# A four-layer graph network on one core: row-by-row fetching by SP and ACT in the two attention sweeps as well, and PSUM operands in the spreading of logits and in two node stages

## The chip, the cores and the metric

One core of one Trainium2 chip runs the whole program in one launch. The metric is the device time of one execution in microseconds.

## What is computed

12,500 nodes with 128 features, 200,000 edges sorted by destination. Four layers, each with a LayerNorm and a ReLU ahead of it and a residual sum behind it: attention with one head (A, followed by a BatchNorm), attention with four heads and edge features (B), a layer that sums edge features and applies three dense layers (C), and a relational layer with eight weight matrices (rel). Cut to what the change touches:

```python
h = x @ W                                   # A and B: attention
e = leaky_relu(a_src[src] + a_dst[dst] (+ a_edge))
ex = exp(e - segment_max(e, dst)[dst])
out = segment_sum(ex / segment_sum(ex, dst)[dst] * h[src], dst)

agg = segment_sum(edge_attr_128, dst)       # C: its sums ride along with sweep A

h = einsum('nd,rdo->rno', x, W_rel)         # rel
out = relu(x @ W_self + b + segment_sum(h[edge_type, src], dst) / deg)
```

## The kernel before

The program is a row of stages; at the end of each, all five engines meet (`finish_stage`: a drain, one semaphore, a wait for all five): graph (indices, table A), spreading A and sweep A, nodes A (softmax ends, BatchNorm, table B), spreading B and sweep B, nodes B (with layer C and the table of rel), sweep rel, nodes rel. In each sweep every one of 200,704 (padded) edges needs the row of its source node from a table in HBM.

**Sweeps.** An edge array has 128 partitions and 1,568 columns. A sweep takes it in 98 groups of 16 columns (NG = 98, GC = 16, in two steps of 8 columns). For each column GpSimd issues one indirect DMA: 128 rows of the table, one per partition, into the tile `edge_rows` (L1077 for A and B, L2036 for rel). The tile is a ring of 5 groups in A and of 6 in B and rel. GpSimd may begin group g when the sums of group g-NS are stored and group g-NS+1 is summed. VectorE adds the groups up one after another (A and B: logits, L1213 to L1233, then the joining of steps, L1190 and L1195; in A also the edge attributes, L1165 and L1173, and the projection of the edge features, L1242 and L1252; rel: L2107 and L2121). ScalarE does the exponentials, and in A 16 scalings of a column (L1131). SP stores the sums of each group (L1111, L2052). In A it also loads, two groups ahead, the 1 MB of edge attributes (L1091) and the features (L1095). Its order in sweep A is fixed: for each g the attributes of g+2, the features of g+2 (which wait until VectorE has used those of g), the store of g (which waits until g is summed).

**Row-by-row fetching.** In sweep rel, GpSimd leaves out the last column of every second group from 7 on (`HELPED`, 45 of the 98 groups). Its 128 rows are fetched by SP and ACT, one DMA per row: `fetch_rows` loads 32 row numbers from SBUF into 32 registers (L1991) and issues 32 DMAs of one row each (L1993, L1994). SP does a quarter 4 groups ahead and one 3 groups ahead, right behind the store of the group; ACT does a quarter 2 groups ahead and one 1 group ahead. VectorE waits for the rows ahead of the group (after L2107). The row numbers stand in `helped_row`, made at the start of nodes B: a copy to float (L1874), a transpose on TensorE (L1942), a copy back to integers (L1878).

**Spreading.** Ahead of sweeps A and B the logit of a destination node, which stands at its first edge, is spread to all its edges by a scan, logit = keep * logit before + logit (L715, one per head). In B, VectorE then adds the edge terms for all heads at once (L755) and sums them along each node by four more scans (L759). All operands lie in SBUF.

**Nodes.** GpSimd gathers each node's sums in 14 chunks of 7 indirect DMAs (L1280). In nodes A and nodes B, `v_join` scales sums and own rows by the softmax factors and adds them (L1373, L1375, L1377); GpSimd may gather chunk k when chunk k-2 is joined. In nodes rel three VectorE instructions (L2154, L2156, L2158) finish a chunk. Here too all operands lie in SBUF.

## Time and profile before

| | us |
|---|---|
| three runs | 7196.33, 7212.66, 7212.68 (median 7212.66) |
| the profiled execution's own time | 7196.47 |
| its span, first to last instruction | 7194.6 |
| busy: GpSimd (POOL) | 5087.8 (71%) |
| busy: VectorE (DVE) | 3425.5 (48%) |
| busy: ScalarE (ACT) | 985.2 (14%) |
| busy: TensorE (PE) | 624.0 (9%) |
| mean granted TensorE clock | 0.54 of full speed |

Span and own time differ by 1.9 us. The busy shares are means over seven stages with different limits, so the stages have to be read apart. The DMA queues on SP and ACT are "q1" and "q10" in the profile, GpSimd's is "q0"; issuing a DMA isn't counted as busy.

### The profile page before, as it was taken

The numbers are of one execution on the slowest core, as the hardware profiler recorded it, in microseconds if no ns is written. First come the engines' busy times: TensorE is split into PE (matmuls) and PEld (weight loads), VectorE is DVE, ScalarE is ACT, GpSimd is POOL, SyncE is SP. The second block draws the span as 40 slices with busy tenths as digits, with TensorE's granted clock in tenths as the row PEclk, the third lists the DMA queues.
The fourth block names the chain that finished last, engine by engine and source line by source line (L and its number), as shares of the span: only waits on it lengthen the run. The fifth ranks groups of instructions, "written<-read, shape, count | busy, mean of one in ns | idle before, by whom it ended". The sixth has DMA issues, their size and how long they took to land. (4 is left out here: it accounts for less than half of the span.)

```text
span 7194.6 us, 39656 instructions
## 1 busy us (share of the span) xinstructions
PE 624.0 (9%) x2403; PEld 426.9 (6%) x2403; DVE 3425.5 (48%) x6202; ACT 985.2 (14%) x3082; POOL 5087.8 (71%) x5295
## 2 busy tenths in 40 slices
PE   1100000000001530000000000058411000000000
PEld 1100000000000420000000000024200000000000
DVE  8466666666666664444444444478322222222223
ACT  2122222222222120000000000056200000000000
POOL 5777777777775577777777777633477777777776
PEclk7555555555555665555555555579755555555555
DMA  5366767676765423333333333345333333333332
GB/s 182 111 213 210 224 210 225 209 226 209 225 209 180 147 98 113 115 115 115 115 115 115 115 115 115 101 160 201 139 107 108 113 108 107 110 110 107 107 112 86
DMA packets 334692, 1044.18 MB, mean 145 GB/s; under 512 B 106489, under 2 KB 128764, under 8 KB 296514
## 3 DMA queue, kind: packets, MB, share of 16 engines
q1 hardware_dynamic: 151986, 668.92, 25.9%
q0 software_dynamic: 173632, 368.42, 20.3%
q10 hardware_dynamic: 8784, 4.31, 0.2%
q14 instruction: 271, 2.22, 0.1%
q8 instruction: 19, 0.31, 0.0%
HBM read 527.27 MB, written 513.96 MB: 145 GB/s over the span
## 5 line engine op out<-in xcount | busy, mean ns | idle before, releaser
L1077 POOL DMA_INDIRECT edge_rows<-table_b,src_i x1568 | 1502.2, 958 | 477.8 <-issue 477.8
L1077 POOL DMA_INDIRECT edge_rows<-table_a,src_i x1568 | 1483.9, 946 | 477.9 <-issue 477.9
L2036 POOL DMA_INDIRECT edge_rows<-table_rel,rel_row x1523 | 1437.0, 944 | 510.3 <-issue 462.8
L2121 DVE TENSOR_TENSOR edge_rows<-edge_rows,ps 128x1024 f32<-128x1024 f32 x195 | 238.0, 1221 | 1386.9 <-DMA edge_rows<-table_rel,rel_row 1383.5
L1213 DVE TENSOR_TENSOR z<-edge_rows,dst_logit 128x16 f32<-128x16 f32 (+1 forms) x196 | 40.9, 209 | 1679.1 <-DMA edge_rows<-table_b,src_i 1026.4
L1195 DVE TENSOR_TENSOR edge_rows<-edge_rows,ps 128x1032 f32<-128x1032 f32 (+1 forms) x390 | 484.2, 1242 | 84.4 <-ACT edge_rows L1131 67.3
L1190 DVE TENSOR_TENSOR ps<-edge_rows,ps 128x1032 f32<-128x1032 f32 (+1 forms) x390 | 485.7, 1245 | 8.6 <-ACT edge_rows L1131 1.9
L1131 ACT ACTIVATE edge_rows<-edge_rows,weight_decay 128x129 f32<-128x129 f32 x1568 | 470.1, 389 | 0.0
L805 PE MATMUL ps<-ident,edge_rows 128*128 128x128 f32 x16 | 3.9, 426 | 3483.2 <-DVE edge_rows L1195 2034.1
L1134 ACT ACTIVATE ps<-weight_decay 128x128 f32<-128x128 f32 x98 | 27.5, 281 | 1893.4 <-DVE weight_decay L1233 1893.4
L2069 ACT ACTIVATE ps<-keep 128x16 f32<-128x16 f32 x98 | 19.6, 201 | 1850.7 <-DVE edge_rows L2121 1847.0
L2107 DVE TENSOR_TENSOR ps<-edge_rows,ps 128x1024 f32<-128x1024 f32 x195 | 239.5, 1228 | 35.9 <-DMA edge_rows<-table_rel,rel_row 29.2
L1246 DVE TENSOR_TENSOR edge_rows<-edge_rows,ps 128x2112 f32<-128x2112 f32 x98 | 230.7, 2354 | 35.3 <-ACT ps L1134 35.3
L1165 DVE TENSOR_TENSOR ps<-edge_rows,ps 128x1024 f32<-128x1024 f32 x195 | 239.5, 1228 | 0.0
L1173 DVE TENSOR_TENSOR edge_rows<-edge_rows,ps 128x1024 f32<-128x1024 f32 x195 | 236.7, 1214 | 0.1
L1127 ACT ACTIVATE weight_decay<-weight_decay 128x16 f32<-128x16 f32 x98 | 21.2, 216 | 1472.1 <-DVE weight_decay L1233 1472.1
L805 PEld LDWEIGHTS ps<-ident,edge_rows 128*128 128x128 f32 x16 | 3.1, 223 | 3483.8 <-issue 2034.4
L1934 PE MATMUL ps<-w_rel,own_part 128*128 128x512 f32 x392 | 196.7, 641 | 2.5 <-DVE rel L1838 1.2
L912 PE MATMUL ps<-ident,edge_rows 128*1 128x128 f32 (+1 forms) x16 | 3.8, 416 | 2037.5 <-DVE edge_rows L1195 2037.5
L1280 POOL DMA_INDIRECT node_sums<-sums_b,sum_row x98 | 102.5, 1046 | 93.5 <-DVE out_b L1377 52.1
L1751 POOL TENSOR_TENSOR x<-x,par 128x896 f32<-128x896 f32 x14 | 29.2, 2084 | 185.2 <-ACT hn L1645 185.2
L510 POOL DMA_INDIRECT piece<-dst_float,q_i x99 | 98.3, 993 | 79.3 <-DVE q_i L532 50.6
(284 smaller groups left out, 3211.9 us busy)
## 6 DMA issues: line engine op xcount, KB each, us to landing
sums_a<-edge_rows SPq DMA_DIRECT2D x98, 2064.0 KB, 8.2
sums_b<-edge_rows SPq DMA_DIRECT2D x98, 1120.0 KB, 4.7
edge_rows<-in_ea SPq DMA_DIRECT2D x98, 1024.0 KB, 11.8
sums_rel<-edge_rows SPq DMA_DIRECT2D x98, 1024.0 KB, 4.1
table_rel<-rel SPq DMA_DIRECT2D x98, 512.0 KB, 3.0
edge_rows<-table_rel ACTq DMA_DIRECT2D x2880, 0.5 KB
edge_rows<-table_rel SPq DMA_DIRECT2D x2880, 0.5 KB
edge_rows<-table_a,src_i POOLq DMA_INDIRECT x1568
```

The lines of the kernel that those rows point to most:

```text
L1077: e.indirect_dma_start(out=rows[:, s, i, 0:L.W], out_offset=None, in_=L.table, in_offset=bass.IndirectOffsetOnAxis(ap=src[:, at:at + 1], a ...
L1131: done = e.activation(R[:, i, 0:NW], R[:, i, 0:NW], ACT.Copy, scale=wd[:, g % 2, 0, i, :])
L1165: attr_step.append(then(e.tensor_tensor(old_attr, before(g, t)[:, :, L.W:L.WS], bc(keep_now[:, t, :].unsqueeze(2), [P, GK, D]), ALU.mult)))
L1173: done = e.tensor_tensor(now, now, old_attr, ALU.add)
L1190: done = then(e.tensor_tensor(heads(old), heads(before(g, t)), bc(decay_now.unsqueeze(3), [P, GK, H, C + 1]), ALU.mult))
L1195: done = e.tensor_tensor(now, now, old, ALU.add)
L1246: t_weight = then(e.tensor_tensor(heads(R), heads(R), bc(factors[:, 0, :, :].unsqueeze(3), [P, GC, H, C + 1]), ALU.mult))
L1280: e.indirect_dma_start(out=self.buf[:, k % self.depth, b, :], out_offset=None, in_=self.sums, in_offset=bass.IndirectOffsetOnAxis(ap=sum_r ...
L1934: done = e.matmul(ps[:, 4 + 2 * (j % 2) + h, 0:half * D], own_part[:, j, :], w_rel[:, h * half:(h + 1) * half, :].rearrange("p r d -> p (r ...
L2036: e.indirect_dma_start(out=rows[:, s, i, :], out_offset=None, in_=table_rel, in_offset=bass.IndirectOffsetOnAxis(ap=rel_row[:, at:at + 1], ...
L2107: e.tensor_tensor(old, before, keep_now, ALU.mult).then_inc(step.sem, 1)
L2121: i = e.tensor_tensor(steps(g)[:, t, :, :], steps(g)[:, t, :, :], old, ALU.add)
```

## The change

**Fetching.** A class `Helped` takes the place of `HELPED`, `fetch_rows`, `help_out` and `place`. Sweep rel keeps its plan. Sweep B gets the same plan for the same 45 groups: SP two pieces of 32 rows (4 and 3 groups ahead), ACT two pieces (3 and 2 groups ahead, behind its exponential and its copy of the edge terms). In sweep A every fifth group from 9 on (18 groups) is helped, by SP alone, in pieces of 43, 43 and 42 rows, 4, 3 and 2 groups ahead. A piece of 43 rows needs two register loads, one of 32 and one of 11. A row is 130 elements in A and 140 in B, against 128 in rel.

```diff
+    helped_a, helped_b = every(5, 9), every(2, 7)
...
+        def fetch(self, e, regs, g, p0, n):
+            if g not in self.place:
+                return
+            h, s = self.place[g], g % self.NS
+            e.wait_ge(*self.stored[s].at(16 * (g // self.NS)))
+            e.wait_ge(*self.summed.at(g - self.NS + 2))
+            for p in range(p0, p0 + n, len(regs)):
+                m = min(len(regs), p0 + n - p)
+                e.load(regs[0:m], self.index[h:h + 1, p:p + m])
+                for i in range(m):
+                    row = e.snap(regs[i])
+                    e.dma_start(self.rows[p + i:p + i + 1, s, LAST, 0:self.W], self.table[bass.ds(row, 1), :]
+                                ).then_inc(self.fetched[h % 3].sem, 16)
...
 (gpsimd of the attention sweeps)
-                for i in range(GC):
+                for i in range(GC - (g in helped.place)):
...
 (sync, behind the store of group g)
+                if L.AE:
+                    helped.fetch(e, regs_sync, g + 4, 0, P // 4)
+                    helped.fetch(e, regs_sync, g + 3, P // 4, P // 4)
+                else:
+                    helped.fetch(e, regs_sync, g + 4, 0, 43)
+                    helped.fetch(e, regs_sync, g + 3, 43, 43)
+                    helped.fetch(e, regs_sync, g + 2, 86, 42)
...
 (scalar, if L.AE)
+                    helped.fetch(e, regs_scalar, g + 3, P // 2, P // 4)
+                    helped.fetch(e, regs_scalar, g + 2, 3 * P // 4, P // 4)
...
 (vector, ahead of the first instruction of group g)
-                e.wait_ge(*gathered[g % NS].at(16 * GC * (g // NS + 1)))
+                e.wait_ge(*gathered[g % NS].at(helped.by_pool[g]))
+                helped.wait(e, g)
```

**Row numbers.** The float copies, transposes (now three) and copies back move from the start of nodes B into the graph stage.

**Spreading.** ScalarE copies `keep` into PSUM; every scan reads it there. In B the scan of a head writes to PSUM, and a VectorE sum per head, `dst_logit <- edge_logit + PSUM`, takes the place of the one sum over all heads. In A, ScalarE waits until the spreading is over before it begins the sweep.

```diff
+            self.near = ps[:, 0:4, :].rearrange("p b v -> p (b v)")[:, 0:EC]
+            self.spread = ps[:, 4:8, :].rearrange("p b v -> p (b v)")[:, 0:EC]
...
+        def s_near(self, e):
+            e.activation(self.near, keep[:, :], ACT.Copy).then_inc(self.keep_near.sem, 1)
...
-                e.tensor_tensor_scan(self.dst_l[:, :, h], keep[:, :], self.dst_l[:, :, h], 0.0, ALU.mult, ALU.add
+                e.tensor_tensor_scan(at if terms is None else self.spread, self.near, at, 0.0, ALU.mult, ALU.add
...
+                    e.tensor_tensor(at, terms[:, :, h], self.spread, ALU.add).then_inc(step.sem, 1)
```

**Nodes.** In nodes A the two factors and the scaled sums are written to PSUM, and the next instruction reads them there; nodes B keeps its form. In nodes rel the mean and the sum with `own_part` are kept in PSUM.

```diff
-            then(e.tensor_tensor(a[:, :, :, 0:C], a[:, :, :, 0:C], bc(of_sums.unsqueeze(3), wide), ALU.mult))
+            then(e.tensor_tensor(part, a[:, :, :, 0:C], bc(by_sums.unsqueeze(3), wide), ALU.mult))
...
-            e.tensor_tensor(out, a[:, :, :, 0:C], b[:, :, :, 0:C], ALU.add).then_inc(self.joined.sem, 1)
+            e.tensor_tensor(out, b[:, :, :, 0:C], part, ALU.add).then_inc(self.joined.sem, 1)
...
-                t = then(e.tensor_tensor(r, r, chunk(own_part, k), ALU.add))
+                t = then(e.tensor_tensor(mean, chunk(own_part, k), mean, ALU.add))
...
-                e.scalar_tensor_tensor(r, r, 0.0, chunk(x, k), ALU.max, ALU.add).then_inc(out_ready.sem, 1)
+                e.scalar_tensor_tensor(r, mean, 0.0, chunk(x, k), ALU.max, ALU.add).then_inc(out_ready.sem, 1)
```

How the order moves at two places. SP in sweep A before, at the stores of groups 4 and 5 (`sums_a` is a store, `in_ea` 128x16x128 the attributes, 128x208 the features):

```order
L1095 DMA feats<-in_ea 128x208 [waits feats_used]
L1111 DMA sums_a<-edge_rows 128x2x2064 [waits attr_summed,edges_summed]
L1091 DMA edge_rows<-in_ea 128x16x128 [waits attr_summed,edges_stored2]
L1095 DMA feats<-in_ea 128x208 [waits feats_used]
L1111 DMA sums_a<-edge_rows 128x2x2064 [waits attr_summed,edges_summed]
```

SP in sweep A now, the stores of groups 4 and 5 and the start of the first piece for group 9:

```order
L1187 DMA sums_a<-edge_rows 128x2x2064 [waits attr_summed,edges_summed]
L1167 DMA edge_rows<-in_ea 128x16x128 [waits attr_summed,edges_stored2]
L1171 DMA feats<-in_ea 128x208 [waits feats_used]
L1187 DMA sums_a<-edge_rows 128x2x2064 [waits attr_summed,edges_summed]
L240 TENSOR_LOAD helped_src [waits edges_summed,edges_stored4]
L242 ISA
L243 DMA edge_rows<-table_a 1x130
```

The same piece at row 32, where the registers are loaded a second time:

```order
L243 DMA edge_rows<-table_a 1x130
L240 TENSOR_LOAD helped_src
L242 ISA
L243 DMA edge_rows<-table_a 1x130
L242 ISA
```

The same piece's last rows, and what comes next on SP: the loads and the store of group 6, and the second piece.

```order
L242 ISA
L243 DMA edge_rows<-table_a 1x130
L1167 DMA edge_rows<-in_ea 128x16x128 [waits attr_summed,edges_stored3]
L1171 DMA feats<-in_ea 128x208 [waits feats_used]
L1187 DMA sums_a<-edge_rows 128x2x2064 [waits attr_summed,edges_summed]
L240 TENSOR_LOAD helped_src [waits edges_summed,edges_stored4]
```

Ahead of the attributes, the features and the store of group 6 there stand now 43 row DMAs and two register loads; the same holds behind the stores of groups 6 and 7, and then again for every fifth group.

VectorE in the spreading of B, before:

```order
L711 COPY dst_logit<-first_logit 128x4 [waits first_logit,dst_logits_loaded,stage_done]
L715 SCALAR_TENSOR_TENSOR dst_logit<-keep,dst_logit 128x1568 [waits vector_step]
L715 SCALAR_TENSOR_TENSOR dst_logit<-keep,dst_logit 128x1568 x3
L752 MEMSET keep 128x8 [waits vector_step]
L755 TENSOR_TENSOR dst_logit<-dst_logit,edge_logit 128x6272 [waits vector_step]
L759 SCALAR_TENSOR_TENSOR edge_logit<-keep,edge_logit 128x1568 [waits vector_step]
L759 SCALAR_TENSOR_TENSOR edge_logit<-keep,edge_logit 128x1568 x3
```

And now (`ps` is PSUM):

```order
L775 COPY dst_logit<-first_logit 128x4 [waits first_logit,dst_logits_loaded,stage_done]
L781 SCALAR_TENSOR_TENSOR ps<-ps,dst_logit 128x1568 [waits vector_step,keep_near]
L786 TENSOR_TENSOR dst_logit<-edge_logit,ps 128x1568 [waits vector_step]
L781 SCALAR_TENSOR_TENSOR ps<-ps,dst_logit 128x1568 [waits vector_step]
L786 TENSOR_TENSOR dst_logit<-edge_logit,ps 128x1568 [waits vector_step]
L781 SCALAR_TENSOR_TENSOR ps<-ps,dst_logit 128x1568 [waits vector_step]
L786 TENSOR_TENSOR dst_logit<-edge_logit,ps 128x1568 [waits vector_step]
L781 SCALAR_TENSOR_TENSOR ps<-ps,dst_logit 128x1568 [waits vector_step]
L786 TENSOR_TENSOR dst_logit<-edge_logit,ps 128x1568 [waits vector_step]
L828 MEMSET keep 128x8 [waits vector_step]
L828 MEMSET ps 128x8
L832 SCALAR_TENSOR_TENSOR edge_logit<-ps,edge_logit 128x1568 [waits vector_step]
```

No scan has two operands in SBUF any more; the one sum of 6,272 elements became four of 1,568, each behind its scan.

## Rows read from the trace of the kernel before

**Rows 1.** Busy time by stretch; columns: stretch, length in us, each engine, PEclk, DMA share, GB/s.
```profile
316.00:2298.00 1982.00, 0.33 (x2) 0.36 (x3) 1220.51 (x1866) 502.50 (x1861) 1483.98 (x1569) 0.50 0.69 215
...
2660.00:4643.00 1983.00, 0.00 (x0) 0.00 (x0) 884.98 (x1274) 45.37 (x195) 1502.80 (x1569) 0.50 0.39 114
...
5122.00:7030.00 1908.00, 50.74 (x197) 43.70 (x198) 492.13 (x416) 19.64 (x98) 1437.01 (x1523) 0.50 0.35 108
```

**Rows 2.** Costliest groups of instructions, GpSimd's gathers.
```profile
L1077 POOL DMA_INDIRECT edge_rows<-table_a,src_i x1568 | 1483.9, 946 | 477.9 <-issue 477.9
...
L1280 POOL DMA_INDIRECT node_sums<-sums_a,sum_row x98 | 110.0, 1122 | 57.2 <-issue 28.3 <-SPq L171 17.6 <-DVE agg L1377 7.4
L1280 POOL DMA_INDIRECT node_sums<-sums_rel,sum_row x98 | 104.0, 1061 | 37.4 <-issue 29.6 <-POOLq L171 7.8
```

**Rows 3.** Timeline, start of sweep B; columns: start us, length us, engine, line.
```profile
2660.87 0.97 POOL L1077 DMA_INDIRECT edge_rows<-table_b,src_i  x1 [0.30 <-issue]
...
2669.95 13.38 DVE L715 TENSOR_TENSOR_SCAN dst_logit<-keep,dst_logit 128x1568 f32<-128x1568 f32 x4
2670.88 3.25 POOL L1077 DMA_INDIRECT edge_rows<-table_b,src_i  x1 [0.30 <-issue]
...
2722.12 0.95 POOL L1077 DMA_INDIRECT edge_rows<-table_b,src_i  x1 [0.30 <-issue]
```

**Rows 4.** Register loads of sweep rel by source line: ns min/median/max.
```profile
L1991 SPq TENSOR_LOAD <-helped_row x90: 3942/4069/4261, 5208.6 to 6933.2; - x90
```

**Rows 5.** Timeline, one group of sweep rel: the row fetching on ACT and SP.
```profile
6003.63 0.40 SPq L2052 DMA_DIRECT2D sums_rel<-edge_rows  x1
...
6008.07 12.80 ACTq L1994 DMA_DIRECT2D edge_rows<-table_rel  x32
6008.47 13.61 SPq L1994 DMA_DIRECT2D edge_rows<-table_rel  x32
```

**Rows 6.** Timeline, two groups in the middle of sweep A.
```profile
507.80 0.18 DVE L1213 TENSOR_TENSOR z<-edge_rows,dst_logit 128x16 f32<-128x16 f32 x1 [12.50 <-DMA edge_rows<-table_a,src_i]
...
518.66 1.24 DVE L1190 TENSOR_TENSOR ps<-edge_rows,ps 128x1032 f32<-128x1032 f32 x1
519.23 0.94 POOL L1077 DMA_INDIRECT edge_rows<-table_a,src_i  x1 [0.30 <-issue]
...
521.26 0.38 SPq L1111 DMA_DIRECT2D sums_a<-edge_rows  x1
...
521.73 0.55 SPq L1091 DMA_DIRECT2D edge_rows<-in_ea  x1
521.78 0.18 DVE L1213 TENSOR_TENSOR z<-edge_rows,dst_logit 128x16 f32<-128x16 f32 x1 [0.54 <-DMA edge_rows<-table_a,src_i]
```

**Rows 7.** Timeline, start of sweep A: SP's issues and a gather.
```profile
316.41 5.87 SPq L1095 DMA_DIRECT2D feats<-in_ea  x1
...
322.91 4.09 SPq L1095 DMA_DIRECT2D feats<-in_ea  x1
...
326.60 3.83 POOL L1077 DMA_INDIRECT edge_rows<-table_a,src_i  x1 [0.30 <-issue]
```

**Rows 8.** Timeline of SP in sweep A: the store of group 5.
```profile
455.35 0.38 SPq L1111 DMA_DIRECT2D sums_a<-edge_rows  x1
```

**Rows 9.** Timeline, the end of sweep A.
```profile
2296.34 1.23 DVE L1195 TENSOR_TENSOR edge_rows<-edge_rows,ps 128x1032 f32<-128x1032 f32 x1
```

**Rows 10.** Timeline, node stage A, GpSimd's gathers.
```profile
2451.03 0.94 POOL L1280 DMA_INDIRECT node_sums<-sums_a,sum_row  x1 [2.06 <-DVE agg L1377]
...
2458.36 1.82 POOL L1280 DMA_INDIRECT node_sums<-sums_a,sum_row  x1 [0.30 <-issue]
```

**Rows 11.** Timeline, start of node stage B.
```profile
4700.47 0.29 DVE L1878 CAST helped_row<-ps 128x128 int32<-128x128 f32 x1 [3.65 <-PE ps L1942]
```

**Rows 12.** Timeline, ScalarE in sweep B.
```profile
2746.38 0.28 ACT L1134 ACTIVATE ps<-weight_decay 128x128 f32<-128x128 f32 x1 [19.52 <-DVE weight_decay L1233]
```

**Rows 13.** Timeline, node stage rel, a gather of GpSimd.
```profile
7131.39 1.81 POOL L1280 DMA_INDIRECT node_sums<-sums_rel,sum_row  x1 [0.30 <-issue]
```

More of the change, by code:

```diff
@@ L1033, in attention_edges @@
         summed = sem_of("edges_summed", NG)
+        helped = Helped(L.name, helped_b if L.AE else helped_a, helped_src[:, 1 if L.AE else 0, :], L.table, L.W, rows, NS,
+                        stored, summed)
+        gathered = [sem_of(f"edges_gathered{i}", helped.all_by_pool(i)) for i in range(NS)]
         def spare(i):
@@ L1358, in v_join @@
             of_sums, of_own = self.ex[:, s, 0, :, :], self.ex[:, s, 1, :, :]
+            if self.near is None:
+                by_sums, by_own, part = of_sums, of_own, a[:, :, :, 0:C]
+            else:
+                if k >= 1:
+                    e.wait_ge(*self.joined.at(k))
+                factors, part = self.near
+                by_sums, by_own = [factors[:, i * JB * H:(i + 1) * JB * H].rearrange("p (j h) -> p j h", h=H)
+                                   for i in range(2)]
             out = self.out_of(k).rearrange("p j (h c) -> p j h c", h=H)
@@ L1987, in nodes_b_stage @@
         return Programs(sync, scalar, gpsimd, vector, tensor)
-    def fetch_rows(e, regs, table, out, of, h, p0, n, fetched):
-        e.load(regs[0:n], helped_row[h:h + 1, p0:p0 + n])
-        for m in range(n):
-            row = e.snap(regs[m])
-            e.dma_start(out[p0 + m:p0 + m + 1, of, GC - 1, :], table[bass.ds(row, 1), :]).then_inc(fetched.sem, 16)
     def edges_rel_stage(local, own_part):
@@ L2019, in edges_rel_stage @@
         summed = sem_of("edges_summed", NG)
+        helped = Helped("rel", helped_b, helped_rel, table_rel, D, rows, NS, stored, summed)
+        gathered = [sem_of(f"edges_gathered{i}", helped.all_by_pool(i)) for i in range(NS)]
         crossing = Crossing("cross", rows[:, (NG - 1) % NS, GC - GK:GC, :], sb("border_state", [P, NV + 1])[:, :],
@@ L2033, in gpsimd @@
                     e.wait_ge(*summed.at(g - NS + 2))
-                for i in range(GC - (g in place)):
+                for i in range(GC - (g in helped.place)):
                     at = natural(g, i)
@@ L2048, in sync @@
             crossing.q_load(e)
-            regs = [e.alloc_register(f"row_sync{m}") for m in range(P // 4)]
             for g in range(NG):
@@ L2064, in scalar @@
             e.dma_start(b_self[:, :], io["d_self_b"].broadcast_to([P, D])).then_inc(self_loaded.sem, 16)
-            regs = [e.alloc_register(f"row_scalar{m}") for m in range(P // 4)]
             for g in range(NG):
@@ L2199, in _ @@
         def _(e):
+            regs_sync.extend(e.alloc_register(f"row_sync{i}") for i in range(32))
             graph.sync(e)
@@ L2217, in _ @@
         def _(e):
+            regs_scalar.extend(e.alloc_register(f"row_scalar{i}") for i in range(32))
             graph.scalar(e)
```

135 lines of the change are left out of this document (81 added, 54 removed).

## The prediction

> **What bounds the kernel now.** I read the busy time by stretch first. In each of the three sweeps GpSimd is the busiest engine: 1,484 of 1,982 us in A, 1,503 of 1,983 in B, 1,437 of 1,908 in rel, while VectorE has 1,221, 885 and 492 [rows 1]. Then the groups of instructions: GpSimd's gathers have hardly any idle time but "issue" [rows 2]. One gather takes (1483.9 + 477.9) / 1568 = 1.25 us of GpSimd. A sweep is 98 times 16 of these, one behind the other, and every gather taken off GpSimd gives back 1.25 us for as long as nothing else becomes late. What else could become late I read from the timeline: in A VectorE needs 13.46 us for a group (from 507.80 to the store at 521.26, which starts as the group is summed), against 20.0 us of gathers [rows 6]; in B its 885 us are 9 us per group [rows 1]; ScalarE in B has waited 19.5 us when its exponential comes [rows 12]. Last I looked for gathers that take longer than the usual 0.94 us: they do so beside VectorE instructions with two operands in SBUF [rows 3, 7, 10, 13].
>
> **Sweep B.** 45 gathers go: 45 x 1.25 = 56.3 us off. The cover: SP and ACT each get one piece of 32 rows per group. From a store's start to the first row pass 6008.47 - 6003.63 = 4.84 us (4.07 of them the register load [rows 4]), and 32 rows take 13.6 [rows 5]: 18.4 us of SP per group. The groups of B will take 15 and 16 gathers in turn, 18.75 and 20.0 us. So it fits, by 0.35 us in the short ones; sweep rel has the same plan and runs at GpSimd's pace (1,908 us for 1,523 gathers, 1.25 each [rows 1]). ACT: 0.5 us for exponential and copy, 4.4 for the load, 12.8 for the rows [rows 5], 17.7 us, and it comes back 1 us ahead of the next exponential. The last rows of a group are out some 19 us before VectorE wants them. Cost: nothing.
>
> **Start of sweep B.** The first 32 gathers of B span 2722.12 - 2660.87 = 61.25 us where 31 x 1.25 = 38.75 are due: 22.5 us lost, all while VectorE scans and sums with both operands in SBUF (a gather beside the scans takes 3.25 us) [rows 3]. A VectorE product with one operand in PSUM (518.66) runs beside a 0.94 us gather (519.23) in sweep A [rows 6]. So the 22.5 us should go. VectorE's own work stays some 34 us (four scans take 13.38 us [rows 3]; eight extra waits 1 or 2 us); meanwhile GpSimd fills two groups of its ring of six, and VectorE, at 9 us per group, catches up inside two. Bounds: 0 if PSUM operands don't free GpSimd, 22.5. I take 22.5.
>
> **Start of sweep A.** One gather of 3.83 us beside the scan [rows 7]: 2.9 us off.
>
> **Nodes A.** Its gathers average 1,122 ns, (1122 - 944) x 98 = 17.4 us too long [rows 2], most of it beside the three joining instructions (1.82 us for one [rows 10]). They get PSUM operands; the sum with the bias does not. And behind it a second limit is near: gather k waits until chunk k-2 is joined, 2.06 us in one place already [rows 10]. Between 0 and 17.4 I take 10.
>
> **Nodes rel.** (1061 - 944) x 98 = 11.5 us [rows 2], one gather per chunk of 1.81 us [rows 13]. No second limit: 11.5 us off.
>
> **Nodes B.** At its start VectorE idles 3.65 us until TensorE has turned the row numbers [rows 11]. That wait moves into the graph stage, where VectorE and TensorE end long before GpSimd. Between 0 and 3.65 I take 3.5.
>
> Without sweep A's fetching this is 56.3 + 22.5 + 10 + 11.5 + 3.5 = 103.8 us off.
>
> **Sweep A, where I part from the plain count.** 18 gathers go, 22.5 us by the count. But here SP does all 128 rows of a group alone, in three pieces behind three stores in a row. Row for row at 0.42 us (13.61 / 32 [rows 5]), a piece of 43 rows is 4.84 + 43 x 0.42 + a second load, of 11 registers. No row has the price of that load. It lies between 0 and the 4.07 us of a load of 32 [rows 4]; I take it in proportion, 4.07 x 11 / 32 = 1.4, plus 0.17 to the next row. Piece: 24.5 us; of 42 rows 24.1. A group takes GpSimd 20 us, so the pieces overrun their groups. The chain of one cycle of five groups is:
> - store of group G-4, then three pieces: 24.5 + 24.5 + 24.1 = 73.0 us;
> - twice, between them, the attributes (0.55) and the features: 2.0;
> - from the last row's issue to landing, as for a gather (519.23 to 521.78 [rows 6]): 2.55;
> - VectorE waits for these rows ahead of group G, then does G and G+1: 2 x 13.46 = 26.9;
> - then SP stores group G+1, and the next first piece starts behind that store.
>
> Sum: 104.4 us for five groups, where GpSimd now needs 79 x 1.25 = 98.7 and before needed 100. So SP and VectorE in turn become the bound of sweep A. GpSimd's ring of five doesn't stop the chain, it only makes GpSimd wait. Place: the store of group 5 stood at 455.35 [rows 8], now 452.4; 17 cycles, then the last one up to the rows (104.4 - 26.9), then four groups of VectorE: 452.4 + 17 x 104.4 + 77.5 + 53.8 = 2358.5. Before, the last group ended at 2296.34 + 1.23 = 2297.6 [rows 9]. Sweep A gets **61 us longer**, not 25 shorter; each microsecond of a cycle is 18.
>
> The Trainium skill ("DMA: Bandwidth & Descriptors", Latency and other measured facts) gives a `tensor_load` a floor of about 600 ns. By that an estimate for 11 registers would be 0.6 + 11 x (4.07 - 0.6) / 32 = 1.8 us instead of 1.4, and the time 21 us more, 7175. The trace has only loads of 32 and can't decide it.
>
> **Sum.** -103.8 + 61 = -43 us. Against the profiled execution's own 7196.5: **7154 us**. That execution lies at the lowest of the three runs, 16 us under their median; the range has room for it.
>
> **Rivals.**
> 1. *GpSimd stays the bound in A* (the plain count): the chain would have to be under 98.7, 1.9 us less per piece. Against: the cadence of rows is the same in all of sweep rel; even a second load for nothing gives back only 4.2 of the 5.7. For: in A ACT issues no rows beside SP, and that might quicken them. Time: 7196.5 - 103.8 - 25.4 = 7067. Chance 0.15.
> 2. *SP's queue is full behind the attributes* (the slower side). Before, features came some 8 us behind the attributes. Where SP runs late they follow at once, and the only two rows like that show the issue of the features held for 5.87 and 4.09 us [rows 7]. Held twice per cycle, that is +8 to +12 us, C = 112 to 116: at 4.09 each, 7154 + 147 = 7301. It decides from 2.4 us per cycle on (18 x 2.4 = 43): then the gain is gone. Against: at those rows the queue still had the loads of the stage's start in it. The Trainium skill (same page, Queues, rings and completion order) says that an SDMA engine consumes a ring's descriptors in order; by it rows issued behind 1 MB of attributes and a 2 MB store wait for these, which is this rival. Chance 0.25.
> 3. *The pieces of sweep B don't fit* (0.35 us of room): rows of 560 bytes at 0.46 us would make SP the bound there as well, and B gains nothing: 7154 + 56 = 7210. Chance 0.07.
> 4. *PSUM operands don't free GpSimd*: 22.5 + 2.9 + 10 + 11.5 stay, 7201. Against: rows 6. Chance 0.05.
>
> **Numbers.** The forecast keeps 0.48. Its own range, with the second load from 0 to 4.07 us, is 7079 to 7298, most of it near 7154. A measurement of this kernel can tell 0.3% (22 us) from no change. Faster: rival 1 and most of the forecast, 0.58. Within: the forecast's upper part, rivals 3 and 4, 0.17. Slower: rival 2 and the forecast's top end, 0.25. The range, 7065 to 7300, takes in rival 1 and rival 2 up to 4 us twice per cycle.
>
> **What would show it.** Right: in sweep A stores of groups 10, 15, 20 some 104 us apart; VectorE waits ahead of every fifth group for a DMA of SP, GpSimd waits 5 to 6 us per cycle, and the sweep lasts some 2,040 us; the load of 11 registers at 1.4 us; the first 32 gathers of B in 39 us; B some 79 us shorter; nodes rel's gathers at 944 ns. Wrong: sweep A at 1,957 us (rival 1); features held for microseconds behind the attributes (rival 2); gathers still at 3 us beside the scans (rival 4).

## The result and the profile after

The changed kernel took **7548.01 us** (median of 4 runs, 7547.14 to 7550.67), the kernel before 7211.25 in the same series (7196.33 to 7212.68): a ratio of **1.0473** [1.0454, 1.0491]. The forecast was 7154 with a range up to 7300, and faster. It is 337 us slower, so the range missed and the sign too. In short: SP fetches its rows in sweep A with register loads that cost far more than the forecast took for them, and everything else in the change did nearly what was expected of it.

First where the time is. The view of the tile `edge_rows` on GpSimd gives the first and the last gather of each sweep (columns: line, count, ns min/median/max, start of the first and the last), for the kernel before:

```profile
L1077 POOL DMA_INDIRECT edge_rows<-table_a,src_i x1568: 940/944/3826, 316.4 to 2276.9; - x196
L1077 POOL DMA_INDIRECT edge_rows<-table_b,src_i x1568: 940/944/6627, 2660.9 to 4639.7; - x196
L2036 POOL DMA_INDIRECT edge_rows<-table_rel,rel_row x1523: 940/944/963, 5122.9 to 7023.6; - x191
L869 POOL DMA_INDIRECT edge_rows<-sums_a,head_row x8: 942/946/1826, 2304.8 to 2314.5; - x8
L869 POOL DMA_INDIRECT edge_rows<-sums_b,head_row x8: 940/944/1376, 4656.6 to 4665.9; - x8
```

and for the changed one:

```profile
L1153 POOL DMA_INDIRECT edge_rows<-table_a,src_i x1550: 941/947/1927, 316.5 to 2681.1; - x194
L1153 POOL DMA_INDIRECT edge_rows<-table_b,src_i x1523: 941/947/997, 3096.6 to 5001.5; - x191
L2105 POOL DMA_INDIRECT edge_rows<-table_rel,rel_row x1523: 941/947/966, 5482.1 to 7386.4; - x191
L943 POOL DMA_INDIRECT edge_rows<-sums_a,head_row x8: 945/946/1831, 2747.2 to 2756.8; - x8
L943 POOL DMA_INDIRECT edge_rows<-sums_b,head_row x8: 943/947/1387, 5018.5 to 5027.7; - x8
```

The stretches between these starts, before and after (the eight gathers of head_row stand at a sweep's end): sweep A 1988.4 and 2430.7, **+442.3**; end of A with node stage A 356.1 and 349.4, -6.7; sweep B 1995.7 and 1921.9, -73.8; end of B with node stage B 466.3 and 463.6, -2.7; sweep rel to the program's end 2071.7 and 2064.5, -7.2. Together +351.9, and the spans differ by 7546.6 - 7194.6 = 352.0. Outside sweep A that is 90.4 us off, where the sum had 103.8. Some 9 us of what is missing are not the change's: in this execution a gather takes 947 ns in the median, in the one before 944, and 3 ns on each of the 1,523 gathers of sweeps B and rel are 4.6 us per sweep (experiment 1 has both at 944). The rest is mostly node stage A. Sweep A got 442 us longer instead of 61.

One cycle of five groups on SP's queue (`helped_src` holds the row numbers; a "piece" is the rows that SP fetches behind one store), timeline of the changed kernel (compare [rows 5], [rows 6], [rows 8]):

```profile
579.09 0.38 SPq L1187 DMA_DIRECT2D sums_a<-edge_rows  x1
585.97 19.61 SPq L243 DMA_DIRECT2D edge_rows<-table_a  x43
605.68 0.56 SPq L1167 DMA_DIRECT2D edge_rows<-in_ea  x1
606.29 2.25 SPq L1171 DMA_DIRECT2D feats<-in_ea  x1
608.63 0.40 SPq L1187 DMA_DIRECT2D sums_a<-edge_rows  x1
620.82 20.84 SPq L243 DMA_DIRECT2D edge_rows<-table_a  x43
641.75 0.55 SPq L1167 DMA_DIRECT2D edge_rows<-in_ea  x1
...
644.58 0.40 SPq L1187 DMA_DIRECT2D sums_a<-edge_rows  x1
656.71 20.25 SPq L243 DMA_DIRECT2D edge_rows<-table_a  x42
677.06 0.56 SPq L1167 DMA_DIRECT2D edge_rows<-in_ea  x1
...
704.86 0.38 SPq L1187 DMA_DIRECT2D sums_a<-edge_rows  x1
```

From store to store of the first piece the cycle is 704.86 - 579.09 = **125.8 us**; the forecast had 104.4. The pieces, from their store to the attributes behind their rows, take 26.6, 33.1 and 32.5 us (forecast 24.5, 24.5, 24.1). Attributes and features between them hold SP 3.0 and 2.8 us (forecast 1.0). From the last row to the next first store 27.8 (forecast 29.45). The differences, 2.1 + 8.6 + 8.4 + 2.0 + 1.8 - 1.7, are the 21 us. The rows keep the cadence of the forecast; what is late is the first row after each store, 6.9, 12.2 and 12.1 us instead of 4.84. The 18 cycles of the sweep are alike, 124.3 to 127.2 us each. The register loads by source line, each in a stretch that holds one or two of them:

```profile
L240 SPq TENSOR_LOAD <-helped_src x1: 6217/6217/6217, 579.6 to 579.6; - x1
...
L240 SPq TENSOR_LOAD <-helped_src x1: 1423/1423/1423, 599.6 to 599.6; - x1
...
L240 SPq TENSOR_LOAD <-helped_src x1: 11494/11494/11494, 609.1 to 609.1; - x1
...
L240 SPq TENSOR_LOAD <-helped_src x1: 2545/2545/2545, 634.5 to 634.5; - x1
...
L240 SPq TENSOR_LOAD <-helped_src x21: 4187/4341/4585, 3500.0 to 3887.9; - x21
L240 ACTq TENSOR_LOAD <-helped_src x21: 2142/2154/2199, 3511.8 to 3899.5; - x21
```

The load of 32 registers behind the store takes 6.2 us in the first piece, 11.49 in the second and 11.44 in the third; the second loads of the pieces take 1.42, 2.55 and 2.33. In sweep B the same load of 32 is 4.3 us on SP and 2.15 on ACT. [Rows 4] had 4.07 as the only price. Who pays is in the view of waits, sweep A of the changed kernel (us in all, times, longest):

```profile
DVE z L1299 <- DMA edge_rows<-table_a: 921.6, 18, 53.1
POOL edge_rows L1153 <- DVE edge_rows L1280: 288.7, 32, 18.3
POOL edge_rows L1153 <- DMA sums_a<-edge_rows: 151.3, 16, 10.4
DVE ps L1250 <- DMA edge_rows<-in_ea: 113.1, 17, 7.1
```

VectorE waits 18 times, once per cycle, for SP's rows, 51 us each time; GpSimd, which had no idle time but "issue" here [rows 2] (time in which the profile shows nothing that it waits for), waits 440 us for VectorE's sums and SP's stores. The start of sweep B went as forecast for GpSimd (its longest gather in sweep B is 1.00 us; beside a scan it was 3.25 before [rows 3]), but VectorE's own work there became longer. Before, one sum over all heads:

```profile
2683.50 6.69 DVE L755 TENSOR_TENSOR dst_logit<-dst_logit,edge_logit 128x6272 f32<-128x6272 f32 x1
```

and in the changed kernel, the first head's scan and sum, the last scans and the first instruction of group 0:

```profile
3105.45 3.43 DVE L781 TENSOR_TENSOR_SCAN ps<-ps,dst_logit 128x1568 f32<-128x1568 f32 x1
3108.91 2.90 DVE L786 TENSOR_TENSOR dst_logit<-edge_logit,ps 128x1568 f32<-128x1568 f32 x1
...
3131.26 13.37 DVE L832 TENSOR_TENSOR_SCAN edge_logit<-ps,edge_logit 128x1568 f32<-128x1568 f32 x4
3144.54 0.20 DVE L1299 TENSOR_TENSOR z<-edge_rows,dst_logit 128x64 f32<-128x64 f32 x1
```

A sum per head takes 2.90 us, the four together 11.6, where the forecast kept VectorE's work at the 34 us of before. The stretch from the copy ahead of the scans to group 0 is 39.4 us instead of 33.8, and group 0 starts 48 us after the first gather instead of 43. GpSimd's ring of six groups hid that. Whether the operand in PSUM or the step over the other heads' elements makes the sums slow isn't shown: both are new in them.

### The profile page after: what moved, and what is told of

Its sections match the earlier page's. It is cut to its first block and busy times, and to the rows that moved or that the text cites. A ratio compares the mean times of both kernels' runs of the same rounds, so it can differ in the third digit from the quotient of the medians.

```text
span 7546.6 us, 64503 instructions
## 1 busy us (share of the span) xinstructions
PE 621.6 (8%) x2405; PEld 422.3 (6%) x2405; DVE 3425.7 (45%) x6210; ACT 988.8 (13%) x3084; POOL 4990.3 (66%) x5232
## 5 line engine op out<-in xcount | busy, mean ns | idle before, releaser
L1153 POOL DMA_INDIRECT edge_rows<-table_a,src_i x1550 | 1467.4, 947 | 898.4 <-issue 458.3
L1153 POOL DMA_INDIRECT edge_rows<-table_b,src_i x1523 | 1440.9, 946 | 465.2 <-issue 465.2
```

Of the source, the lines that this page charges most:

```text
L1153: e.indirect_dma_start(out=rows[:, s, i, 0:L.W], out_offset=None, in_=L.table, in_offset=bass.IndirectOffsetOnAxis(ap=src[:, at:at + 1], a ...
```

## The experiments

Two kinds of chips came up. Three series ran where the kernel before takes 8847 to 8934 us, two where it takes 7197, close to the first result (7211). Ratios are therefore always against the kernel before in the same series; the mechanism is read from traces of both. The changed kernel itself was never run on the second kind. "Cuts at 48, 88" means pieces of 48, 40 and 40 rows instead of 43, 43 and 42; "loads early" means that SP reads the row numbers ahead of the attributes, the features and the store; h3 is a single run. Medians in us, and the ratio with its interval:

| kernel | before at 7197 | before at 8847 to 8934 |
|---|---|---|
| changed kernel (g1) | 7541.20, 1.0478 [1.0457, 1.0498] | |
| no rows in A (i1; e1, f1, h1) | 7094.33, 0.9857 [0.9841, 0.9874] | 9858, 9755, 9751: 1.1040 [1.1022, 1.1059], 1.1015 [1.0996, 1.1033], 1.1019 [1.1001, 1.1037] |
| no rows in A and B (g3) | 7149.23, 0.9933 [0.9916, 0.9949] | |
| no rows at all (i4) | 7204.78, 1.0011 [1.0002, 1.0021] | |
| A, loads early (e2, f2) | | 11107, 10918: 1.2441 [1.2421, 1.2462], 1.2322 [1.2301, 1.2343] |
| A, cuts at 48, 88 (g2) | 7312.01, 1.0159 [1.0139, 1.0179] | |
| A, cuts at 48, 88, loads early (g4) | 7136.52, 0.9915 [0.9895, 0.9935] | |
| A on two queues (i2; e3, f3, h2) | 7069.34, 0.9823 [0.9806, 0.9839] | 10494, 10377, 10366: 1.1751 [1.1731, 1.1771], 1.1718 [1.1699, 1.1738], 1.1713 [1.1693, 1.1733] |
| A on two queues, loads early (i3) | 7071.84, 0.9826 [0.981, 0.9842] | |
| ACT's load of B at the store (h3) | | 9956, beside 9751 of h1 |

**1. Is it all sweep A?** The fetching there is taken out and nothing else.

```diff
-        helped = Helped(L.name, helped_b if L.AE else helped_a, ...
+        helped = Helped(L.name, helped_b if L.AE else {}, ...
```

> The change without the row fetching in sweep A: GpSimd gathers all 16 columns there again; sweep B, sweep rel and the PSUM operands stay as changed. Theory (all of the loss comes from the fetching in sweep A, which the trace shows 442 us longer from its first gather to the border's): 7548 - 442 = 7106 us, between 7095 and 7120; sweep A at 1,988 us again. Rival (part of the loss is outside sweep A, or the sweep's other new parts cost there too, the spreading from PSUM ahead of it): above 7150.

> Once more the kernel without the row fetching in sweep A, because the chip of the first series took 8934 us for the kernel before instead of 7211, with SP's rows 0.87 us apart instead of 0.44. On a chip where the kernel before takes 7211 us, all of the loss in sweep A: 7106 us, 7095 to 7120. Rival, part of the loss elsewhere: above 7150.

> The change without the row fetching in sweep A, on what I expect to be a chip like the one of the third series (kernel before 7197 us, changed kernel 7541). All of the loss in sweep A: the kernel with neither fetching took 7149; sweep B from its first gather to the border's took 1973 us there and 1920 with fetching, so 7149 - 53 = 7096, between 7085 and 7110. Rival (the trace of one stretch misleads, B's fetching gives less in the whole): 7120 or more.

> The change without the row fetching in sweep A, for a chip on which the kernel before takes some 7200 us: 7096, 7085 to 7110 (7149 of the kernel with neither fetching, less the 53 us by which sweep B is shorter with it). Rival: 7120 or more. On a chip on which the kernel before takes some 8850: a ratio of 1.10 as in the three series there.

The first three fell on the other kind of chip, where the kernel came out 10% slower than before, and told nothing of this question. The fourth gave 7094.33 where 7096 was expected. Its sweeps (same view as above):

```profile
L1153 POOL DMA_INDIRECT edge_rows<-table_a,src_i x1568: 940/944/2445, 316.0 to 2273.9; - x196
L1153 POOL DMA_INDIRECT edge_rows<-table_b,src_i x1523: 940/944/998, 2649.4 to 4550.3; - x191
L2105 POOL DMA_INDIRECT edge_rows<-table_rel,rel_row x1523: 940/944/961, 5032.3 to 6932.7; - x191
L943 POOL DMA_INDIRECT edge_rows<-sums_a,head_row x8: 944/946/1826, 2301.9 to 2311.5; - x8
L943 POOL DMA_INDIRECT edge_rows<-sums_b,head_row x8: 940/945/1377, 4567.3 to 4576.5; - x8
```

Against before: sweep A 1985.9 (-2.5), node stage A 347.5 (-8.6), sweep B 1917.9 (-77.8), node stage B 465.0 (-1.3), rel to the end 2060.0 (-11.7): 101.9 us, where the sum had 103.8 and 2.9 for the start of A. So the whole loss is the fetching in sweep A: against the kernel before, everything else gains 102 us.

**2. The PSUM operands alone**, with the fetching taken out of both attention sweeps (`Helped(L.name, {}, ...)`).

> The change without the fetching in sweeps A and B: only the operands in PSUM (spreading of logits, nodes A, nodes rel) and the moved turning are left; sweep rel is fetched as before. By the traces before and after: start of B 22, start of A 3, nodes A 7 to 8, nodes rel 11, nodes B 3, so 46 us off: 7165 us on a chip where before takes 7211 (7155 to 7180), a ratio of 0.993 to 0.995 on any chip. Rival (the operands in PSUM give back nothing where sweep B hides its start): 7190 to 7215.

It took 7149.23 beside 7197.25, 48 us less (by the interval 37 to 60). Sweep B there was 1973.1 us from its first gather to the border's: 22.6 under before for the start, and 55.2 over i1 for the 45 gathers. Both terms, 22.5 and 56.3, hold.

**3. Why is the load slow?** Two ways to move it: earlier, and to another place of the array. First earlier:

```diff
+    PIECES = (4, 0, 43), (3, 43, 43), (2, 86, 42)
...
             for g in range(NG):
+                if not L.AE:
+                    for a, p0, n in PIECES:
+                        helped.read(e, regs_sync, g + a, p0, n)
                 if g + 2 < NG:
                     load(g + 2)
...
+                    for a, p0, n in PIECES:
+                        helped.fetch(e, regs_sync, g + a, p0, n, False)
```

> Sweep A as changed, but SP reads the row numbers of a piece into registers (43 registers, loads of 32 and 11) before it issues the attributes, the features and the store of that round, not behind them. Theory 1 (a register load takes long because bulk transfers are in flight when it is issued): the loads of pieces 2 and 3 fall from 11 to about 4 us, the first piece's come to lie in SP's idle time; the cycle of five groups falls from 125.8 to some 103 us, 18 x 22 = 400 us off, total 7150, between 7110 and 7200. Theory 2 (a load in sweep A is slow whatever is ahead of it, by the many small rows just issued or by where the numbers lie): loads of pieces 2 and 3 still near 11 us, only the first piece's 7.7 us per cycle leave the chain, 18 x 7.7 = 139 us off, total 7410.

> Once more the change with SP's register loads ahead of the attributes, the features and the store. Theory 1 (a load takes long because bulk transfers are in flight when it is issued): loads of pieces 2 and 3 about 4 us instead of 11, cycle of five groups some 103 us, total 7150, 7110 to 7200. Theory 2 (slow whatever is ahead of it): still near 11, only the first piece's loads leave the chain, total 7410.

The totals (1.24 and 1.23) can't be held against the expected ones, since the chips were the other kind. The loads can. From e2's trace, by source line, the first piece (start 1257.8) and the second (1335.8), each the load of 32 and the second load:

```profile
L236 SPq TENSOR_LOAD <-helped_src x1: 6143/6143/6143, 1257.8 to 1257.8; - x1
...
L237 SPq TENSOR_LOAD <-helped_src x1: 1174/1174/1174, 1264.0 to 1264.0; - x1
...
L236 SPq TENSOR_LOAD <-helped_src x1: 6735/6735/6735, 1335.8 to 1335.8; - x1
...
L237 SPq TENSOR_LOAD <-helped_src x1: 2275/2275/2275, 1342.5 to 1342.5; - x1
```

The second piece's load has neither store nor attributes ahead of it, and takes 6.73 us: neither theory's number (4 or 11). The loads of 11 pointed to another cause: 1.17 us when they start at row 32, 2.28 from row 75, 0.21 us per register there, and 6.73 / 32 = 0.21 too. The register loads of sweeps B and rel all start at multiples of 32 rows, those of the slow pieces at 43 and 86. A row number has 4 bytes, so multiples of 8 rows are multiples of 32 bytes. So in the next series the cuts were moved to such places:

```diff
-                    helped.fetch(e, regs_sync, g + 4, 0, 43)
-                    helped.fetch(e, regs_sync, g + 3, 43, 43)
-                    helped.fetch(e, regs_sync, g + 2, 86, 42)
+                    helped.fetch(e, regs_sync, g + 4, 0, 48)
+                    helped.fetch(e, regs_sync, g + 3, 48, 40)
+                    helped.fetch(e, regs_sync, g + 2, 88, 40)
```

> The changed kernel itself, to stand beside the other runs of this series on the same chip. On a chip where the kernel before takes 7211 us: 7548. On one like those of the two series so far (kernel before 8850 to 8930, rows of SP about 0.87 us apart, with stretches in which every instruction of SP takes 0.70 us): the kernel without fetching in A stood at a ratio of 1.10 to before there, the one with early loads at 1.23 to 1.24, so 1.24 to 1.27 here. Its loads in sweep A: 6.3, 11.2 and 10.8 us for 32 registers as in the profile of the changed kernel, on either kind of chip.

> Sweep A as changed, but its pieces are cut at rows 48 and 88 instead of 43 and 86, so that every register load starts at a multiple of 32 bytes (loads of 32 and 16, 32 and 8, 32 and 8 registers). In the run with early loads the loads of 32 from rows 43 and 86 took 6.73 us with no bulk transfer ahead of them, the 11 from row 32 took 1.17, the 11 from row 75 took 2.28. Theory A (where the read starts decides, about 0.2 us per register from an uneven place and 0.1 from an even one): behind the store the loads of 32 of pieces 2 and 3 take 6.2 to 7 instead of 11.2 and 10.8, the second loads of 8 about 1 us instead of 2.4; the cycle is 11 us shorter, the total 7548 - 18 x 11 = 7340 on a chip like the first, and some 200 us under the changed kernel on any. Theory B (only the bulk transfers and rows in flight decide): loads of pieces 2 and 3 stay at 10.5 to 11.5 us, the total within 40 us of the changed kernel's.

> Both: pieces cut at rows 48 and 88, and SP's register loads ahead of the attributes, the features and the store. Theory A (place of the read and bulk in flight add up): loads of 32 of pieces 2 and 3 fall to 2.2 us, what ACT's loads take in sweep B with nothing beside them; that of piece 1, still right behind a 2 MB store, stays at 6.2 in SP's idle time. The cycle of five groups comes down to GpSimd's 98.7 us or a few above on a chip like the first (total 7080 to 7130), and on a chip with rows 0.87 us apart to some 45 us under the changed kernel's cycle. Theory B (the rows in flight decide, not the place): 6.7 us stays for pieces 2 and 3.

g4 is e2 with these cuts. The cuts alone gave 7312 beside 7541 on the same chip, 229 us less. The register loads account for it: the six of the cycle shown above take 35.4 us in the changed kernel, the six of the cycle below 22.6, and 18 x 12.8 = 230. The loads of 32 of one cycle of g2 (three pieces), then the first two of g4 (the third is as the second, 2.13; neither has a store just ahead of it):

```profile
L240 SPq TENSOR_LOAD <-helped_src x1: 6417/6417/6417, 1125.9 to 1125.9; - x1
...
L240 SPq TENSOR_LOAD <-helped_src x1: 6468/6468/6468, 1157.5 to 1157.5; - x1
...
L240 SPq TENSOR_LOAD <-helped_src x1: 6872/6872/6872, 1185.4 to 1185.4; - x1
```

```profile
L236 SPq TENSOR_LOAD <-helped_src x1: 6417/6417/6417, 1057.1 to 1057.1; - x1
...
L236 SPq TENSOR_LOAD <-helped_src x1: 2128/2128/2128, 1093.7 to 1093.7; - x1
```

Two prices add up: a load of 32 registers takes **2.13 us**, **4.6 more** if it starts at row 43 or 86 instead of 48 or 88 (6.73), and **4.1 to 4.7 more** right behind a 2 MB store (6.2 to 6.9 in g2); together they make 10.8 to 11.4, beside 10 to 12.2 in the changed kernel. The 6.73 and the 2.13 are from different kinds of chip, but on one chip (g1 beside g2) the loads of 32 of the second and third piece went from 11.5 and 10.7 us to 6.6 and 6.9 in the median, which is the same step. Theory A held. This cycle was 1125.9 - 1014.0 = 111.9 us in g2 and 1057.1 - 955.4 = 101.7 in g4, the mean of all cycles 113 and 103. That is still over GpSimd's 98.7, and g4's total (7137, expected 7080 to 7130) stays 42 us over the kernel without fetching in A.

Does a load wait for the store because it is behind it in SP's queue, or because the store is under way? One kernel, without fetching in A, lets ACT's load in sweep B, from a queue without a store, start with SP's store:

```diff
+                    if g + 3 in helped.place or g + 2 in helped.place:
+                        e.wait_ge(*summed.at(g + 1))
                     helped.fetch(e, regs_scalar, g + 3, P // 2, P // 4)
```

> The kernel without fetching in A, and in sweep B ACT waits, ahead of its fetching, until the group is summed, so that its register load starts together with SP's 1.1 MB store, which is on another engine's queue. In the changed kernel ACT's loads in sweep B take 2.15 us with no store beside them, SP's behind the store 4.1 to 4.3, and in sweep rel, where ACT's load starts with SP's store, 4.1 on both. Theory (what is in flight decides, whosever queue it is in): ACT's loads of sweep B now take 4.0 to 4.3 us. Rival 1 (a load waits for its own engine's queue): they stay at 2.15. Rival 2 (the array helped_rel of sweep rel is the slow one, by its place): they stay at 2.15 too. Either way each group of B becomes longer, since ACT comes back late: 26 us by the theory, 24 by the rivals, instead of 19.4, so some 400 to 650 us on top of the kernel without fetching in A.

```profile
L240 SPq TENSOR_LOAD <-helped_src x90: 3644/4174/4512, 3091.7 to 6226.9; - x90
L240 ACTq TENSOR_LOAD <-helped_src x90: 2128/4207/4605, 3109.8 to 6261.9; - x90
...
L240 ACTq TENSOR_LOAD <-helped_src x1: 4081/4081/4081, 6261.9 to 6261.9; - x1
```

ACT's median is 4.21 us. In h1, on the same chip and without the edit, it was 2.69 (from 0.70 to 4.36), where ACT's loads meet a store only in part of the groups, and 2.15 in the changed kernel. SP's own register load starts at the same moment, so it could be that one load slows the other; the last line shows the one load of ACT that started with a store and with no load of SP beside it, and it took 4.08. On a chip of the first kind it shows as well: in i2 (below) ACT's second load of a cycle starts some 5 us behind SP's 2 MB store and takes 3.7 us in the median, in i3, on the same chip, where the next store comes 7 us later, 2.15. The store under way is what counts, in whichever queue. (The total rose by 205 us and not by 400 or more; on that chip ACT's rows are slow in any case, so the total, from a single run, decides nothing.)

A fourth kernel, again without fetching in A, was meant to time the loads without rows:

```diff
+                    for a, p0, n in ((4, 0, 43), (3, 43, 43), (2, 86, 42)):
+                        if g + a in helped_a:
+                            h = helped_a[g + a]
+                            e.load(regs_sync[0:32], helped_src[h:h + 1, 0, p0:p0 + 32])
+                            e.load(regs_sync[0:n - 32], helped_src[h:h + 1, 0, p0 + 32:p0 + n])
```

> The kernel without fetching in A, but with SP's six register loads per cycle of five groups (32 and 11, 32 and 11, 32 and 10) left in behind the three stores; no rows are fetched from them, GpSimd gathers all columns. SP has no rows to issue, so it is on time and the attributes are long landed when the store is issued. Theory 1 (a load takes as long as the bulk ahead of it is in flight): every load of 32 takes about 6.2 us behind its 2 MB store, none 11, the second ones 1.4 or less. Theory 2 (11 us come from sweep A's place or from something else than late attributes): pieces 2 and 3 at 11 us here as well. Theory 3 (the rows of the piece before are what a load waits for): 4.1 us everywhere. Total as the kernel without fetching in A by either.

Its one run took 9881.88, as the kernel without fetching in A (9858.27), and its trace has no register load in sweep A, presumably because nothing reads these registers. It decided nothing.

**4. The overrun, or any fetching in A?** Sweep A gets sweep B's plan: two pieces of 32 on SP and two on ACT.

```diff
-                    helped.fetch(e, regs_sync, g + 4, 0, 43)
-                    helped.fetch(e, regs_sync, g + 3, 43, 43)
-                    helped.fetch(e, regs_sync, g + 2, 86, 42)
+                    helped.fetch(e, regs_sync, g + 4, 0, P // 4)
+                    helped.fetch(e, regs_sync, g + 3, P // 4, P // 4)
...
+                if not L.AE:
+                    helped.fetch(e, regs_scalar, g + 3, P // 2, P // 4)
+                    helped.fetch(e, regs_scalar, g + 2, 3 * P // 4, P // 4)
```

> Sweep A fetched by the plan of sweep B: SP two pieces of 32 rows (behind the stores of groups g-4 and g-3), ACT two pieces of 32 (behind the exponentials of g-3 and g-2), still every fifth group. Theory (SP's overrun of its groups is what costs; two short pieces of at most 11 + 13.6 us are caught up in the other three groups, and ACT's 2.2 + 12.8 us fit into 20): GpSimd stays the bound at 98.7 us per five groups, the total is that of the kernel without fetching in A less 18 x 1.25 = 22.5, about 7083, between 7065 and 7110. Rival (every late attribute transfer of sweep A reaches VectorE and the ring, also with short pieces, or ACT's rows hold its exponential): 2 to 7 us per cycle on top, 7110 to 7210.

> Once more sweep A by the plan of sweep B, pieces of 32 rows, two on SP and two on ACT. Theory (SP's overrun of its groups is what costs): 7083 us, 7065 to 7110, 22 us under the kernel without fetching in A. Rival (late attributes or a late exponential still cost 2 to 7 us per cycle): 7110 to 7210.

> Sweep A by the plan of sweep B: pieces of 32 rows at rows 0, 32, 64 and 96, two on SP and two on ACT, still every fifth group. SP's cycle is no longer a chain of three overrun groups: 6.2 + 13.6 us of load and rows and some 3 us of attributes and features in two groups of 20 us, a few us late and caught up in the other three. Theory (only the overrun costs): 22 us under the kernel without fetching in A, 7074, between 7060 and 7090. Rival (a store or an attribute transfer that is late at all reaches the ring or VectorE, or ACT's rows hold its exponential): 0 to 7 us per cycle, 7096 to 7200.

> Sweep A by the plan of sweep B, pieces of 32 rows from rows 0 and 32 on SP and from 64 and 96 on ACT. Where before takes some 7200 us: 7074, 7060 to 7090, if only the overrun of three pieces in a row costs; ACT has 5.2 us of weighting, 2.2 of load and 12.8 of rows, 20.2 against a group of 20. Rival (late stores and attributes reach the ring or VectorE all the same): 7096 to 7200. Where before takes some 8850: a ratio of 1.17 as there.

> The same plan on two queues, but SP reads the row numbers of its piece before the attributes, the features and the store. SP's second piece is then 2.1 us of load instead of 6.2 or more. Theory (GpSimd is the bound either way): the same as with late loads within 5 us, 7074. Rival (SP's lateness still costs there): 4 us per cycle less than with late loads, up to 70 us.

7069.34 and 7071.84, where 7074 was expected. GpSimd's gathers and its waits in sweep A, i2:

```profile
L1153 POOL DMA_INDIRECT edge_rows<-table_a,src_i x1550: 940/944/1988, 316.3 to 2251.4; - x194
L943 POOL DMA_INDIRECT edge_rows<-sums_a,head_row x8: 944/947/1822, 2277.9 to 2287.6; - x8
```

```profile
POOL edge_rows L1153 <- issue: 439.5, 1442, 0.3
```

Sweep A is 2277.9 - 316.3 = 1961.6 us, 24.3 under the kernel without rows there (22.5 by the count of gathers), and GpSimd is back to "issue" alone. In A, too, fetching pays where the pieces are short and on two queues. The plan changes the cuts and the share per queue at once; g4, with good cuts and early loads but three pieces on SP, still has sweep A 37 us longer than without rows (2022.8 beside 1985.9), so the cuts alone are not enough. Early loads on top (i3) change nothing. The version on two queues (i2) beats both kernels on chips of the first kind: 1.8% under before (its interval leaves out 1), 6.3% under the changed one by the two ratios.

**5. No rows at all** (`Helped("rel", {}, ...)` as well).

> No rows are issued by SP or ACT in any sweep, GpSimd gathers all 16 columns everywhere; the operands in PSUM stay. Where before takes some 7200 us: sweep rel loses its 45 x 1.25 = 56 us, 7149 + 56 = 7205, a ratio of 1.000 to 1.002. Where before takes some 8850: theory (the instructions of the rows, four to a row, are what such a chip supplies too slowly): the sweeps go at GpSimd's 1.25 us per gather again, 7250 to 7450 us, a ratio of 0.82 to 0.84. Rival (such a chip is slow in everything, rows or not): a ratio of 0.97 or more.

It landed on a chip of the first kind: 7204.78, where 7205 was expected. Beside the 7149.23 of g3 the rows of sweep rel are worth the 56 us of their 45 gathers there. What it would take on the other kind was not tried.

## Why the prediction was wrong

**The step that failed** is the size of the register loads in the term of sweep A, "a piece of 43 rows is 4.84 + 43 x 0.42 + a second load, of 11 registers": 4.07 us were taken for a load of 32 wherever it stands, from SP's only row that had one [rows 4]. That row was a load from a multiple of 32 with a 1 MB store under way. Sweep A's are behind 2 MB, and two of three start at a row that is no multiple of 8: 6.2, 11.5 and 11.4 us. Over a cycle the three loads of 32 cost 16.9 us more than counted and the second loads 2.1 (1.42, 2.55, 2.33 for 3 x 1.4). Attributes and features, a second term that was too small, add 3.8; from the last row to the next store the cycle gives back 1.7. That is the 21 us per cycle, 18 cycles of it 382 us; 61 + 382 = 443 beside the measured 442.3. (By the prices of experiment 3, 2 x 4.6 = 9.2 of the 16.9 are the place where the loads start, and the rest is nearly all the larger store.)

**The chain was right.** SP's pieces, landing, two groups of VectorE and the next store are what bounds sweep A; VectorE's 18 waits are where the forecast put them, and GpSimd waits as forecast but 24 us per cycle instead of 5 to 6. With loads, attributes and features at their measured length the same sum gives the sweep. I had written that "each microsecond of a cycle is 18"; the range then let only the second load vary, from 0 to 4.07, and never the first, which occurs three times a cycle and had no row taken in its conditions.

**Rival 2** (features held behind attributes, C = 112 to 116) had the right side, slower, and was right that SP's late transfers cost more than on time: the features were held 2.1 and 2.3 us between the pieces, not 4.09 to 5.87. The 3.8 us per cycle are above the 2.4 from which, as the rival says, the gain is gone; alone they would have given 7154 + 68 = 7222. That is a fifth of the excess of 21 us. Its number, 7301, was passed by another cause.

**Rival 1** (GpSimd stays the bound in A) fell for this plan and is what i2 shows for the other one (7069 beside its 7067). **Rival 3** fell, though its condition came true: in sweep B SP needs 5.26 us from a store to the first row (3806.24 to 3811.50 in g1) instead of 4.84, more than the 0.35 us of room in the short groups; the long ones make up for it, and GpSimd's idle time in sweep B is "issue" alone. **Rival 4** fell.

**The other terms**, forecast and measured (i1 and g3 against before): sweep B's rows 56.3 and 55.2; start of B 22.5 and 22.6; start of A 2.9 and 2.5; nodes A 10 and 8.6 (6.7 in the changed kernel; the second limit that I named was there, VectorE's joins held GpSimd 10 to 18 us instead of 7.4 [rows 2]); nodes rel with sweep rel 11.5 and 11.7; nodes B 3.5 and 1.3.

**The estimate by the Trainium skill** ("DMA: Bandwidth & Descriptors", Latency and other measured facts) had put 1.8 us for 11 registers, from a floor of about 600 ns. Measured: 1.17 to 1.42 from row 32, 2.28 to 2.55 from row 75, so neither 1.4 nor 1.8 was the one price; and the loads of 8 in g4 take 0.53 us, a little under that floor.

## What to carry to other kernels

When a term is multiplied by the number of cycles, ask of its price whether the row that gave it stood in the same conditions: here the size of the store under way and the place from which the read starts, each worth a factor of two to three. Work that is moved to a queue must fit between two of that queue's own duties at the worst price seen, not the mean; two short pieces on each of two queues made sweep A 24 us shorter, three long ones on one queue made it 442 us longer. And where a split is free, cut it at multiples of 32 bytes (48/40/40 rows for 43/43/42 gave back 229 us). Last, a gain from work on such queues has to be measured on more than one chip.

## What the runs showed of the hardware

- A register load (32 numbers of 4 bytes from SBUF) took 2.13 to 2.15 us from rows 48, 64, 88 and 96 (g4) and 6.73 us or slightly more from rows 43 and 86 (e2), with no store just ahead. Loads of 16 and 8 took 0.98 and 0.53 (0.06 to 0.07 us per register), the 11 from row 75 took 2.28 (0.21 each), the 11 from row 32 1.17, which is 8 at 0.067 and 3 at 0.21. The Trainium skill ("Runtime: NRT & Kernel Launch", Instruction fetch mechanics) gives about 200 ns per register, even in bulk, for loads from HBM. The loads here are from SBUF: those from rows that are no multiple of 8 agree with it (0.21), the others don't. That a read from a multiple of 32 bytes goes eight numbers at a time is only argued from these sums, and the slow starts are 12 (rows 43 and 75) and 24 bytes (row 86) past such a place; others were not tried.
- The same load took about 2 us more with a 1.0 to 1.1 MB store under way, on SP's queue (4.07, 4.3) or ACT's (h3: 4.21), and 4.1 to 4.7 more right behind a 2 MB store on its own queue (g2).
- Chips differ in how fast SP and ACT get through their instructions. The same kernel (no rows in A), 32 rows of SP on a chip of the other kind, and all its row issues on either:

```profile
4004.43 28.21 SPq L243 DMA_DIRECT2D edge_rows<-table_b  x32
```

```profile
L243 SPq DMA_DIRECT2D edge_rows<-table_b x2880: 2/225/1407, 3094.2 to 6127.3; - x192
```

```profile
L243 SPq DMA_DIRECT2D edge_rows<-table_b x2880: 224/228/341, 2745.3 to 4483.6; - x192
```

28.2 us for 32 rows instead of 13.6 [rows 5]; the median issue is the same 0.225 us, but single ones take up to 1.41, where the other chip's stay under 0.35. Each row is three instructions of its queue. The kernels with more rows lost more there: 1.10 with rows in B and rel, 1.17 with A's on two queues, 1.24 with A's on SP alone. So the best version here, with its rows in all three sweeps, is 17% slower than the kernel before on those chips. Row fetching isn't all of it: sweep A of e1 and h1, which has no rows, lasts 2240 and 2229 us from its first gather to the border's, where i1 has 1986; sweep B of e1, with rows, 3173 where i1 has 1918. What makes these chips so, and what a kernel without any rows would take there, stays open.
